# Another order of the same calls in the step functions of VectorE, ScalarE and GpSimd

## The chip, the cores and the metric

One Trainium2 chip, one core. The metric is the device time of one execution in microseconds.

## The reference

Tokens are 8 sequences of 2048 rows with 512 channels, float32. First an attention-like recurrence with a residual and a layer norm, then a gated feed-forward with token shift, a residual and a second layer norm:

```
rkv = x @ W_rkv + b_rkv;  r, k, v = split(rkv)
k = exp(k);  kv = k * v
y = associative_scan(y[t] = lam * y[t-1] + [kv, k][t]);  u1, u2 = split(y)
a = (u1 + gamma * kv) / (u2 + gamma * k + 1e-6) * sigmoid(r)
x = layernorm(x + a @ W_o + b_o)
x_prev = x shifted by one token, zero at the start of a sequence
xr = mu_r * x + (1 - mu_r) * x_prev;  xk = mu_k * x + (1 - mu_k) * x_prev
o = sigmoid(xr @ W_r.T) * (square(relu(xk @ W_k.T)) @ W_v.T)
out = layernorm(x + o)
```

## The kernel before

The 16384 tokens are worked in 32 blocks of 512. A block's attention part is computed with channels on the partitions, in four chunks of 128 channels (`c` = 0 to 3), and its feed-forward part in two halves of 256 tokens (`half` 0 and 1), tiles of 128 tokens with tokens on the partitions. Every operand of a product is held as a high part (`_hi`, rounded by ScalarE) and a low part (`_lo`, the difference, by VectorE or GpSimd), and each product is three matmuls: high by high, high by low, low by high. A projection is 12 matmuls (L787 to L789) into one of four banks `bankA`; the output, receptance and value products (L804 to L806), the transposes (L830) and the key products (L852 to L854) go into four banks `bankB`, taken in a fixed rotation (`SLOTS`): each product waits until the engine that reads the one four slots before it is done.

The work is pipelined by hand: a step `s` holds the attention part of block `s`, the output product and most of the feed-forward part of block `s - 1` (`s1`), and the value product of half 1 with the last norm of block `s - 2` (`s2`). Each of the five engines has its own `step` function that says in which order it calls the pieces; they synchronise by semaphores alone. Steps 0 to 2 are straight code, then a hardware loop runs over batches 1 to 7 with four steps in its body, then step 31, `last_block` and `last_half`. An engine takes its instructions in the order written; one that waits holds up all behind it.

TensorE's step is: projections of chunk 0; value product of half 1 of `s2`; output products of `s1` (four tiles); first projection of chunk 1; two transposes of half 0; the rest of chunks 1 and 2; two transposes of half 1; receptance and key products of half 0; projections of chunk 3; value, receptance and key products of half 0, 1 and 1.

The pieces that the change moves, and what they wait for:

- ScalarE: `exp_key` (L434) and `exp_gate` (L440, L443) read a projection; `att_high` (L447) waits for GpSimd's `att`; `copy_zT` (L455) empties two transposes' banks; `previous_scaled` (L463) makes eight chunks from `zT`; `mixed_high` (L483) waits for VectorE's `mix`; `normalise` (L470) waits for GpSimd's `inverse_std` (`shift`, L334); `tanh` (L495) empties a receptance bank; `key_square` (L505 to L509) empties a key bank and makes `ka_f`, `ka_hi`; `x_high` (L415) waits for the load of the next block's `xT`.
- VectorE: `denominator` (L633 to L651), `numerator` (L659 to L664), `attention_rows` (L685), `statistics` (L671, L677), `mix` (L694), `key_low` (L702), `gated_values` (L710), `x_low` (L607).
- GpSimd: `att` (L316), `att_low` (L320), `inverse_std` (L325 to L334), `mixed_low` (L341), `residual` (L347), `bias_rows` (L353), and in step 0 `weight_low` (L311).
- SyncE's queue issues the loads and stores in a fixed order: store of half 1 of `s2` (after its `normalise`), row loads of half 1, `xT` of block `s + 1` (after the last projection), row loads of half 0, store of half 0 of `s1`.

Of the kernel before, what the change touches and what calls it, by code (L numbers as in the profile page):

```python
# [86 lines left out]
def program(nc, xT, x, w_rkv, w_o, w_r, w_k, w_v, b_rkv, b_o, nu_log, gamma_log, mu_r, mu_k, out, seq):  # L87
# [9 lines left out]
    with ExitStack() as ctx:  # L97
# [199 lines left out]
        def _(pool):  # L297
# [57 lines left out]
            def step(s):  # L355
                s1, s2 = s.back(1), s.back(2)
                first = s.batch is None and s.s == 0
                if s2.exists():
                    residual(s2, 1)
                if s1.exists():  # L360
                    inverse_std(s1, 0, 0)
                if s2.exists():
                    inverse_std(s2, 1, 1)
# [8 lines left out]
                att(s, 1)  # L372
                att_low(s, 1)
                if first:
                    weight_low(W_R)
                att(s, 2)
                att_low(s, 2)
                if first:
                    weight_low(W_K)
                if s1.exists():  # L380
                    mixed_low(s1, 1, s)
                    residual(s1, 0)
                att(s, 3)
# [3 lines left out]
                if s1.exists():  # L387
                    inverse_std(s1, 1, 0)
                bias_rows(s)

            def last_block(s):
                s1, s2 = s.back(1), s.back(2)
# [16 lines left out]
        def _(act):  # L409
# [116 lines left out]
            def step(s):  # L526
                s1 = s.back(1)
# [8 lines left out]
                if s.back(2).exists():  # L536
                    normalise(s.back(2), 1, 1, result_rows(s.back(2)), out_made)
                if s1.exists():
                    copy_zT(s1, 0)
                    normalise(s1, 0, 1, z_rows(s1), z_made)  # L540
                    previous_scaled(s1, 0, s)
                att_high(s, 0)
                exp_gate(s, 1)
                if first:
                    weight_high(W_R)
                if s1.exists():
                    mixed_high(s1, 0, s)
                exp_key(s, 2)
# [12 lines left out]
                exp_key(s, 3)  # L561
# [5 lines left out]
                if s.back(-1).exists() and not first:  # L567
                    x_high(s.back(-1))
                att_high(s, 3)
                if s1.exists():  # L570
                    normalise(s1, 1, 0, result_rows(s1), out_made)
                    tanh(s1, 1)
                    key_square(s1, 1)

            def last_block(s):
                s1, s2 = s.back(1), s.back(2)
# [379 lines left out]
```

## Time and profile before

| | |
|---|---|
| median of 3 runs | 2697.14 us (2694.0 to 2699.29) |
| profiled execution, its own time | 2699.09 us |
| its span | 2697.3 us |
| mean granted TensorE clock | 0.987 |
| instructions | 36409 |

The profile is one execution. Its page gives each engine's busy time; the waits say who waited for whom and how long; the timeline lists instructions in order of time, those that follow each other at the same line in one row; the windows give busy time and the granted clock in a stretch. Idle time of an engine that doesn't bound the kernel costs nothing by itself.

### The profile page before, as it was taken

How to read it: one execution, taken by the hardware profiler on the slowest of the kernel's cores; microseconds unless marked ns; L12 is line 12 of the kernel's file. 1: busy time of each engine (PE TensorE's matmuls, PEld its weight loads, DVE VectorE, ACT ScalarE, POOL GpSimd, SP SyncE). 2: the span in 40 equal slices, each digit the busy share in tenths (PEclk: the TensorE clock that was granted, in tenths of full speed). 3: DMA queues.
4: the chain of work that ended last, by engine and by line, in shares of the span. 5: the costliest groups of instructions: out<-in, count | busy, mean ns of one | idle time of the engine just before them, and what ended most of it. 6: DMA issues, size and time to landing. Idle time of an engine off the chain costs nothing.

```text
span 2697.3 us, 36409 instructions
## 1 busy us (share of the span) xinstructions
PE 2560.1 (95%) x12800; PEld 2166.3 (80%) x12800; DVE 2045.1 (76%) x2826; ACT 1287.5 (48%) x2255; POOL 1293.9 (48%) x1166
## 2 busy tenths in 40 slices
PE   7899999999999999999999999999999999999997
PEld 5788888878888888888888888888888888888886
DVE  8877778777778777877777777777877777777773
ACT  4445454544454444545454544445454444545454
POOL 3545454454554454454544544545445454454453
PEclk8999999999999999999999999999999999999998
DMA  4001111011010011110111100111101111101010
GB/s 168 16 32 48 32 48 40 24 48 48 32 48 32 33 47 36 44 40 27 46 48 32 48 32 32 47 32 48 40 24 47 48 33 40 39 32 47 32 32 24
DMA packets 57800, 110.89 MB, mean 41 GB/s; under 512 B 7040, under 2 KB 7040, under 8 KB 57088
## 3 DMA queue, kind: packets, MB, share of 16 engines
q1 hardware_dynamic: 57600, 108.31, 12.1%
q8 instruction: 115, 1.88, 0.3%
q14 instruction: 85, 0.70, 0.1%
HBM read 74.73 MB, written 33.55 MB: 40 GB/s over the span
## 4 chain that ended last, share of the span: by engine, by line
PE 47%; DVE 20%; ACT 13%; issue 12%; POOL 7%; DMA 1%; SPq 0%; DVEq 0%; ACTq 0%; POOLq 0%
PE bankB L804 8%; PE bankB L806 7%; PE bankB L805 7%; PE bankA L787 5%; PE bankA L789 5%; PE bankA L788 5%; DVE gate L648 4%; DVE x_lo L607 4%; POOL att_f L316 4%; PE bankB L852 3%; PE bankB L853 3%; PE bankB L854 3%; DVE att_f L659 3%; ACT t L470 2%; ACT xr_f L463 2%
## 5 line engine op out<-in xcount | busy, mean ns | idle before, releaser
L787 PE MATMUL bankA<-x_hi,wrkv_hi 128*128 128x512 f32 x1536 | 606.7, 395 | 26.2 <-DVE x_lo L607 11.4
L788 PE MATMUL bankA<-x_lo,wrkv_hi 128*128 128x512 f32 x1536 | 602.5, 392 | 0.0
L789 PE MATMUL bankA<-x_hi,wrkv_lo 128*128 128x512 f32 x1536 | 601.9, 392 | 0.0
L651 DVE RECIPROCAL gate<-gate 128x512 f32<-128x512 f32 x128 | 429.2, 3353 | 4.4
L316 POOL TENSOR_TENSOR att_f<-att_f,gate 128x512 f32<-128x512 f32 x128 | 205.2, 1603 | 381.5 <-DVE att_f L664 380.7
L320 POOL TENSOR_TENSOR att_lo<-att_f,att_hi 128x512 fp32r<-128x512 f32 x128 | 205.8, 1608 | 358.2 <-ACT att_hi L447 358.2
L787 PEld LDWEIGHTS bankA<-x_hi,wrkv_hi 128*128 128x128 f32 x1536 | 291.1, 190 | 87.8 <-issue 23.1
L852 PE MATMUL bankB<-xk_hi,wk_hi 128*128 128x256 f32 x1024 | 297.4, 290 | 64.7 <-ACT zT L455 58.9
L702 DVE TENSOR_TENSOR ka_lo<-ka_f,ka_hi 128x512 fp32r<-128x512 f32 x128 | 104.6, 817 | 334.4 <-ACT ka_f L509 334.4
L789 PEld LDWEIGHTS bankA<-x_hi,wrkv_lo 128*128 128x128 f32 x1536 | 290.8, 189 | 61.6
L347 POOL TENSOR_TENSOR t<-t,y 128x512 f32<-128x512 f32 x128 | 191.2, 1514 | 304.3 <-DVE t L710 304.3
L788 PEld LDWEIGHTS bankA<-x_lo,wrkv_hi 128*128 128x128 f32 x1536 | 291.1, 190 | 57.1
L447 ACT ACTIVATE att_hi<-att_f 128x512 fp32r<-128x512 f32 x128 | 80.1, 626 | 474.3 <-POOL att_f L316 474.3
L470 ACT ACTIVATE y<-y,shift,rstd 128x512 f32<-128x512 f32 x128 | 97.2, 810 | 436.8 <-POOL shift L334 436.7
L853 PE MATMUL bankB<-xk_lo,wk_hi 128*128 128x256 f32 x1024 | 294.0, 287 | 0.0
L854 PE MATMUL bankB<-xk_hi,wk_lo 128*128 128x256 f32 x1024 | 293.7, 287 | 0.0
L852 PEld LDWEIGHTS bankB<-xk_hi,wk_hi 128*128 128x128 f32 x1024 | 200.4, 196 | 79.8 <-ACT zT L455 76.3
L804 PE MATMUL bankB<-wv_hi,ka_hi 128*128 128x512 f32 x512 | 201.4, 393 | 19.3 <-DVE ka_lo L702 18.5
L341 POOL TENSOR_TENSOR xr_lo<-xr_f,xr_hi 128x1024 fp32r<-128x1024 f32 x64 | 166.6, 2603 | 110.3 <-ACT xr_hi L483 110.0
L804 PE MATMUL bankB<-wo_hi,att_hi 128*128 128x512 f32 x512 | 201.1, 393 | 11.9 <-POOL att_lo L320 9.9
L804 PE MATMUL bankB<-wr_hi,xr_hi 128*128 128x512 f32 x512 | 202.0, 395 | 0.0
L853 PEld LDWEIGHTS bankB<-xk_lo,wk_hi 128*128 128x128 f32 x1024 | 200.9, 196 | 1.2
(88 smaller groups left out, 5720.3 us busy)
## 6 DMA issues: line engine op xcount, KB each, us to landing
x_f<-in_xT SPq DMA_DIRECT2D x128, 256.0 KB, 4.0
y<-in_x SPq DMA_DIRECT2D x128, 256.0 KB, 2.7
out<-t SPq DMA_DIRECT2D x128, 256.0 KB, 2.0
wrkv_f<-in_w_rkv SPq DMA_DIRECT2D x3, 768.0 KB, 6.3
wo_f<-in_w_o SPq DMA_DIRECT2D x1, 1024.0 KB, 9.7
wr_f<-in_w_r SPq DMA_DIRECT2D x1, 1024.0 KB, 11.6
wk_f<-in_w_k SPq DMA_DIRECT2D x1, 1024.0 KB, 13.6
wv_f<-in_w_v SPq DMA_DIRECT2D x1, 1024.0 KB, 15.6
```

Of the source, the lines that this page charges most:

```text
L316: pool.tensor_tensor(att_f[:, c], att_f[:, c], gate[:, c % 2], ALU.mult).then_inc(att_made, 1)
L320: pool.tensor_tensor(att_lo[:, c], att_f[:, c], att_hi[:, c], ALU.subtract).then_inc(att_lo_made, 1)
L347: pool.tensor_tensor(t[:, tile], t[:, tile], y[:, y_slot(s, tile)], ALU.add).then_inc(y2_made, 1)
L651: dve.reciprocal(gate[:, c % 2], gate[:, c % 2]).then_inc(rec_made, 1)
L787: pe.matmul(bank[:], w_hi, x_hi[:, h], start=(h == 0), stop=False)
L788: pe.matmul(bank[:], w_hi, x_lo[:, h], start=False, stop=False)
L789: last = pe.matmul(bank[:], w_lo, x_hi[:, h], start=False, stop=(h == NC - 1))
L804: pe.matmul(bank[:], hi, w_hi[:, c], start=(c == 0), stop=False)
L805: pe.matmul(bank[:], hi, w_lo[:, c], start=False, stop=False)
L852: pe.matmul(dst, wk_hi[:, c, cols], xk_hi[:, c], start=(c == 0), stop=False)
L853: pe.matmul(dst, wk_hi[:, c, cols], xk_lo[:, c], start=False, stop=False)
L854: last = pe.matmul(dst, wk_lo[:, c, cols], xk_hi[:, c], start=False, stop=(c == NC - 1))
```

## The change

The `step` and `last_block` functions of VectorE, ScalarE and GpSimd call the same pieces with the same arguments in another order. SyncE's functions are untouched. TensorE's `step` has its loops over `which` written out as three calls each, in the same order. No instruction is added or removed. The tuple's parentheses and `(not first)` in the diff change nothing and are left out below, as is the text of TensorE's.

```diff
 GpSimd
             def step(s):
+                if s1.exists():
+                    inverse_std(s1, 0, 0)
                 if s2.exists():
                     residual(s2, 1)
-                if s1.exists():
-                    inverse_std(s1, 0, 0)
-                if s2.exists():
-                    inverse_std(s2, 1, 1)
                 if s1.exists():
                     inverse_std(s1, 0, 1)
                 att(s, 0)
...
                 att(s, 1)
+                if s2.exists():
+                    inverse_std(s2, 1, 1)
                 att_low(s, 1)
                 if first:
                     weight_low(W_R)
                 att(s, 2)
+                if s1.exists():
+                    mixed_low(s1, 1, s)
+                    residual(s1, 0)
                 att_low(s, 2)
                 if first:
                     weight_low(W_K)
-                if s1.exists():
-                    mixed_low(s1, 1, s)
-                    residual(s1, 0)
                 att(s, 3)
+                if s1.exists():
+                    inverse_std(s1, 1, 0)
                 att_low(s, 3)
                 if first:
                     weight_low(W_V)
-                if s1.exists():
-                    inverse_std(s1, 1, 0)
                 bias_rows(s)
             def last_block(s):
                 inverse_std(s1, 0, 0)
                 residual(s2, 1)
+                inverse_std(s2, 1, 1)
                 inverse_std(s1, 0, 1)
-                inverse_std(s2, 1, 1)
 ScalarE
             def step(s):
...
                     normalise(s1, 0, 0, z_rows(s1), z_made)
                 exp_key(s, 1)
-                if s.back(2).exists():
-                    normalise(s.back(2), 1, 1, result_rows(s.back(2)), out_made)
                 if s1.exists():
                     copy_zT(s1, 0)
-                    normalise(s1, 0, 1, z_rows(s1), z_made)
                     previous_scaled(s1, 0, s)
-                att_high(s, 0)
+                    mixed_high(s1, 0, s)
                 exp_gate(s, 1)
                 if first:
                     weight_high(W_R)
-                if s1.exists():
-                    mixed_high(s1, 0, s)
+                att_high(s, 0)
                 exp_key(s, 2)
+                if s1.exists():
+                    normalise(s1, 0, 1, z_rows(s1), z_made)
                 exp_gate(s, 2)
+                if s1.exists():
+                    copy_zT(s1, 1)
                 att_high(s, 1)
                 if first:
                     weight_high(W_K)
                 if s1.exists():
-                    copy_zT(s1, 1)
+                    key_square(s1, 0)
+                if s.back(2).exists():
+                    normalise(s.back(2), 1, 1, result_rows(s.back(2)), out_made)
+                if s1.exists():
+                    previous_scaled(s1, 1, s)
+                exp_key(s, 3)
+                if s1.exists():
                     tanh(s1, 0)
-                    key_square(s1, 0)
-                    previous_scaled(s1, 1, s)
-                if first:
-                    x_high(s.back(-1))
-                att_high(s, 2)
-                exp_key(s, 3)
                 exp_gate(s, 3)
                 if first:
                     weight_high(W_V)
                 if s1.exists():
                     mixed_high(s1, 1, s)
-                if s.back(-1).exists() and not first:
+                att_high(s, 2)
+                if first:
+                    x_high(s.back(-1))
+                if s.back(-1).exists() and (not first):
                     x_high(s.back(-1))
                 att_high(s, 3)
                 if s1.exists():
-                    normalise(s1, 1, 0, result_rows(s1), out_made)
                     tanh(s1, 1)
                     key_square(s1, 1)
+                    normalise(s1, 1, 0, result_rows(s1), out_made)
             def last_block(s):
                 normalise(s1, 0, 0, z_rows(s1), z_made)
                 copy_zT(s1, 0)
                 previous_scaled(s1, 0, s)
+                mixed_high(s1, 0, s)
+                normalise(s2, 1, 1, result_rows(s2), out_made)
                 normalise(s1, 0, 1, z_rows(s1), z_made)
-                normalise(s2, 1, 1, result_rows(s2), out_made)
-                mixed_high(s1, 0, s)
                 copy_zT(s1, 1)
                 key_square(s1, 0)
+                previous_scaled(s1, 1, s)
                 tanh(s1, 0)
-                previous_scaled(s1, 1, s)
                 mixed_high(s1, 1, s)
+                normalise(s1, 1, 0, result_rows(s1), out_made)
                 key_square(s1, 1)
                 tanh(s1, 1)
-                normalise(s1, 1, 0, result_rows(s1), out_made)
 VectorE
             def step(s):
...
                     attention_rows(s1, 0)
-                if s2.exists():
-                    statistics(s2, 1, 1, result_rows(s2), y2_made)
-                if s1.exists():
                     attention_rows(s1, 1)
                 numerator(s, 0)
                 if s1.exists():
                     mix(s1, 0, s)
                 denominator(s, 1)
+                if s2.exists():
+                    statistics(s2, 1, 1, result_rows(s2), y2_made)
                 numerator(s, 1)
...
-                if first:
-                    x_low(s.back(-1))
                 denominator(s, 3)
                 if s1.exists():
                     gated_values(s1, 0)
+                if first:
+                    x_low(s.back(-1))
...
             def last_block(s):
                 attention_rows(s1, 0)
                 gated_values(s2, 1)
-                attention_rows(s1, 1)
                 statistics(s2, 1, 1, result_rows(s2), y2_made)
                 mix(s1, 0, s)
+                attention_rows(s1, 1)
```

Where the instructions stand, at three places. First ScalarE in step 3, from the end of `exp_gate(s, 2)` to `exp_key(s, 3)`, before:

```order
L443 ACTIVATE gate<-gate 128x512
L447 ACTIVATE att_hi<-att_f 128x512
L455 ACTIVATE zT<-bankB 128x2x256 x2
L495 ACTIVATE t<-bankB 128x512 x2
L505 ACTIVATE ka_f<-bankB 128x512
...
L463 ACTIVATE xr_f<-zT,om_mu 128x256 x4
L463 ACTIVATE xk_f<-zT,om_mu 128x256 x4
L447 ACTIVATE att_hi<-att_f 128x512
L434 ACTIVATE key<-bankA,b_sb 128x512
```

and of the change:

```order
L443 ACTIVATE gate<-gate 128x512
L455 ACTIVATE zT<-bankB 128x2x256 x2
L447 ACTIVATE att_hi<-att_f 128x512
L505 ACTIVATE ka_f<-bankB 128x512
...
L470 ACTIVATE t<-t,shift,rstd 128x512 x2
L463 ACTIVATE xr_f<-zT,om_mu 128x256 x4
L463 ACTIVATE xk_f<-zT,om_mu 128x256 x4
L434 ACTIVATE key<-bankA,b_sb 128x512
L495 ACTIVATE t<-bankB 128x512 x2
```

The copy of the transposed rows (`zT`) moved ahead of `att_hi`; tanh (`t` from `bankB`) moved from behind the copy to behind `key`; the scaling of two result tiles (L470) came in ahead of the eight chunks.

Second, ScalarE at the end of the same step, before:

```order
L415 ACTIVATE x_hi<-x_f 128x512 x4
L447 ACTIVATE att_hi<-att_f 128x512
L470 ACTIVATE t<-t,shift,rstd 128x512 x2
L495 ACTIVATE t<-bankB 128x512 x2
L505 ACTIVATE ka_f<-bankB 128x512
```

and of the change:

```order
L415 ACTIVATE x_hi<-x_f 128x512 x4
L447 ACTIVATE att_hi<-att_f 128x512
L495 ACTIVATE t<-bankB 128x512 x2
L505 ACTIVATE ka_f<-bankB 128x512
...
L470 ACTIVATE t<-t,shift,rstd 128x512 x2
```

The scaling of the half's two result tiles went from ahead of tanh and the squares to the end of the step.

Third, VectorE in step 0, from the end of `numerator(s, 2)` to the end of `denominator(s, 3)`, before:

```order
L664 SCALAR_TENSOR_TENSOR att_f<-kv,gamma,att_f 128x512
L607 TENSOR_TENSOR x_lo<-x_f,x_hi 128x512 x4
L633 SCALAR_TENSOR_TENSOR u<-lam,key 128x512
L638 SCALAR_TENSOR_TENSOR kv<-bankA,b_sb,key 128x512
...
L651 RECIPROCAL gate<-gate 128x512
```

and of the change:

```order
L664 SCALAR_TENSOR_TENSOR att_f<-kv,gamma,att_f 128x512
L633 SCALAR_TENSOR_TENSOR u<-lam,key 128x512
L638 SCALAR_TENSOR_TENSOR kv<-bankA,b_sb,key 128x512
...
L651 RECIPROCAL gate<-gate 128x512
L607 TENSOR_TENSOR x_lo<-x_f,x_hi 128x512 x4
```

The low parts of the next block's `xT` went from ahead of the last denominator to behind it.

## Rows read from the trace of the kernel before

**Rows 1.** The page, part 1: busy time, share of the span, instructions of each engine.

```profile
PE 2560.1 (95%) x12800; PEld 2166.3 (80%) x12800; DVE 2045.1 (76%) x2826; ACT 1287.5 (48%) x2255; POOL 1293.9 (48%) x1166
```

**Rows 2.** TensorE's waits: engine, line, who ended them; us, times, longest.

```profile
PE bankB L852 <- ACT zT L455: 58.9, 31, 2.1
PE bankB L804 <- DVE ka_lo L702: 18.5, 23, 0.8
```

**Rows 3.** Timeline of TensorE: start, duration (us), line, operation, [idle before it].

```profile
1377.61 0.40 PE L787 MATMUL bankA<-x_hi,wrkv_hi 128*128 128x512 f32 x1
...
1386.73 0.47 PE L804 MATMUL bankB<-wv_hi,ka_hi 128*128 128x512 f32 x1 [0.77 <-DVE ka_lo L702]
...
1426.48 0.39 PE L806 MATMUL bankB<-wr_hi,xr_lo 128*128 128x512 f32 x1
1428.83 0.38 PE L852 MATMUL bankB<-xk_hi,wk_hi 128*128 128x256 f32 x1 [1.96 <-ACT zT L455]
...
1434.67 0.40 PE L787 MATMUL bankA<-x_hi,wrkv_hi 128*128 128x512 f32 x1
...
1442.86 0.39 PE L804 MATMUL bankB<-wv_hi,ka_hi 128*128 128x512 f32 x1
...
1453.74 0.28 PE L852 MATMUL bankB<-xk_hi,wk_hi 128*128 128x256 f32 x1
...
1459.49 0.40 PE L787 MATMUL bankA<-x_hi,wrkv_hi 128*128 128x512 f32 x1
```

**Rows 4.** Timeline of ScalarE and GpSimd, same step, around the key products.

```profile
1419.30 2.85 POOL L341 TENSOR_TENSOR xk_lo<-xk_f,xk_hi 128x1024 fp32r<-128x1024 f32 x1
...
1427.66 0.63 ACT L447 ACTIVATE att_hi<-att_f 128x512 fp32r<-128x512 f32 x1 [5.73 <-POOL att_f L316]
1428.19 1.07 ACT L455 ACTIVATE zT<-bankB 128x512 f32<-128x512 f32 x2
...
1436.71 1.70 ACT L463 ACTIVATE xr_f<-zT,om_mu 128x256 f32<-128x256 f32 x4
...
1439.91 0.62 ACT L447 ACTIVATE att_hi<-att_f 128x512 fp32r<-128x512 f32 x1
```

**Rows 5.** Timeline of ScalarE and VectorE before the value product of half 1.

```profile
1379.74 1.52 ACT L470 ACTIVATE t<-t,shift,rstd 128x512 f32<-128x512 f32 x2 [2.71 <-POOL shift L334]
1381.16 1.06 ACT L495 ACTIVATE t<-bankB 128x512 f32<-128x512 f32 x2
...
1385.89 0.69 DVE L702 TENSOR_TENSOR ka_lo<-ka_f,ka_hi 128x512 fp32r<-128x512 f32 x1 [0.64 <-ACT ka_f L509]
```

**Rows 6.** Windows over key products: busy PE, PEld, DVE, ACT, POOL; PEclk; DMA.

```profile
1263.00:1271.00 8.00, 7.39 (x49) 7.40 (x50) 6.82 (x6) 3.88 (x8) 2.98 (x2) 0.79 0.00 0
...
1346.00:1353.00 7.00, 6.07 (x49) 6.05 (x50) 6.86 (x7) 4.21 (x9) 2.16 (x2) 1.00 0.01 2
```

**Rows 7.** Timeline of VectorE in step 0, TensorE's output product in step 1.

```profile
31.80 5.15 DVE L648 SCALAR_TENSOR_TENSOR gate<-key,gate 128x512 f32<-128x512 f32 x1 [1.46 <-ACT gate L443]
...
57.91 0.69 DVE L607 TENSOR_TENSOR x_lo<-x_f,x_hi 128x512 fp32r<-128x512 f32 x1 [1.36 <-ACT x_hi L415]
59.01 1.82 DVE L633 TENSOR_TENSOR_SCAN u<-lam,key 128x512 f32<-128x512 f32 x1 [0.41 <-ACT key L434]
...
75.38 0.79 PE L804 MATMUL bankB<-wo_hi,att_hi 128*128 128x512 f32 x1 [9.88 <-POOL att_lo L320]
```

**Rows 8.** Timeline of TensorE at the begin of the last block.

```profile
2619.39 0.64 PE L804 MATMUL bankB<-wo_hi,att_hi 128*128 128x512 f32 x1 [2.06 <-ACT ka_f L505]
```

**Rows 9.** Timeline of VectorE: the low parts of the next block's input.

```profile
1449.66 5.12 DVE L607 TENSOR_TENSOR x_lo<-x_f,x_hi 128x512 fp32r<-128x512 f32 x4
```

**Rows 10.** Timeline of GpSimd and VectorE at the same time.

```profile
1416.52 2.82 POOL L341 TENSOR_TENSOR xr_lo<-xr_f,xr_hi 128x1024 fp32r<-128x1024 f32 x1
...
1417.12 2.77 DVE L648 SCALAR_TENSOR_TENSOR gate<-key,gate 128x512 f32<-128x512 f32 x1
```

**Rows 11.** Timeline of GpSimd: the product of chunk 1.

```profile
1425.43 2.19 POOL L316 TENSOR_TENSOR att_f<-att_f,gate 128x512 f32<-128x512 f32 x1 [3.29 <-DVE att_f L664]
```

More of the change, by code:

```diff
@@ L355, in step @@
             def step(s):
-                s1, s2 = s.back(1), s.back(2)
+                s1, s2 = (s.back(1), s.back(2))
                 first = s.batch is None and s.s == 0
-                if s2.exists():
-                    residual(s2, 1)
                 if s1.exists():
@@ L362, in step @@
                 if s2.exists():
-                    inverse_std(s2, 1, 1)
+                    residual(s2, 1)
                 if s1.exists():
@@ L379, in step @@
                     weight_low(W_K)
+                att(s, 3)
                 if s1.exists():
-                    mixed_low(s1, 1, s)
-                    residual(s1, 0)
-                att(s, 3)
+                    inverse_std(s1, 1, 0)
                 att_low(s, 3)
@@ L386, in step @@
                     weight_low(W_V)
-                if s1.exists():
-                    inverse_std(s1, 1, 0)
                 bias_rows(s)
             def last_block(s):
-                s1, s2 = s.back(1), s.back(2)
+                s1, s2 = (s.back(1), s.back(2))
                 inverse_std(s1, 0, 0)
                 residual(s2, 1)
+                inverse_std(s2, 1, 1)
                 inverse_std(s1, 0, 1)
-                inverse_std(s2, 1, 1)
                 mixed_low(s1, 0, s)
@@ L545, in step @@
                     weight_high(W_R)
+                att_high(s, 0)
+                exp_key(s, 2)
                 if s1.exists():
-                    mixed_high(s1, 0, s)
-                exp_key(s, 2)
+                    normalise(s1, 0, 1, z_rows(s1), z_made)
                 exp_gate(s, 2)
+                if s1.exists():
+                    copy_zT(s1, 1)
                 att_high(s, 1)
@@ L570, in step @@
                 if s1.exists():
-                    normalise(s1, 1, 0, result_rows(s1), out_made)
                     tanh(s1, 1)
                     key_square(s1, 1)
+                    normalise(s1, 1, 0, result_rows(s1), out_made)
             def last_block(s):
-                s1, s2 = s.back(1), s.back(2)
+                s1, s2 = (s.back(1), s.back(2))
                 normalise(s1, 0, 0, z_rows(s1), z_made)
@@ L716, in step @@
             def step(s):
-                s1, s2 = s.back(1), s.back(2)
+                s1, s2 = (s.back(1), s.back(2))
                 first = s.batch is None and s.s == 0
@@ L742, in step @@
                     gated_values(s1, 0)
-                if s.back(-1).exists() and not first:
+                if first:
+                    x_low(s.back(-1))
+                if s.back(-1).exists() and (not first):
                     x_low(s.back(-1))
@@ L750, in last_block @@
             def last_block(s):
-                s1, s2 = s.back(1), s.back(2)
+                s1, s2 = (s.back(1), s.back(2))
                 attention_rows(s1, 0)
                 gated_values(s2, 1)
-                attention_rows(s1, 1)
                 statistics(s2, 1, 1, result_rows(s2), y2_made)
                 mix(s1, 0, s)
+                attention_rows(s1, 1)
                 key_low(s1, 0)
@@ L865, in step @@
             def step(s):
-                s1, s2 = s.back(1), s.back(2)
-                for which in range(3):
-                    project(s, 0, which)
+                s1, s2 = (s.back(1), s.back(2))
+                project(s, 0, 0)
+                project(s, 0, 1)
+                project(s, 0, 2)
                 if s2.exists():
@@ L878, in step @@
                 project(s, 1, 2)
-                for which in range(3):
-                    project(s, 2, which)
+                project(s, 2, 0)
+                project(s, 2, 1)
+                project(s, 2, 2)
                 if s1.exists():
@@ L884, in step @@
                     keys(s1, 0, s)
-                for which in range(3):
-                    project(s, 3, which)
+                project(s, 3, 0)
+                project(s, 3, 1)
+                project(s, 3, 2)
                 if s1.exists():
@@ L892, in last_block @@
             def last_block(s):
-                s1, s2 = s.back(1), s.back(2)
+                s1, s2 = (s.back(1), s.back(2))
                 attention_out(s1, 0, s)
```

## The prediction

> **What bounds the kernel now.** I read the page first: TensorE is busy 95% of the span, VectorE 76%, ScalarE and GpSimd 48% each [rows 1]. A new order on the three others can win only what TensorE stands idle, 137 us, plus what its stalls cost around them. So the next view is who ends TensorE's waits. Two groups recur in every step: 58.9 us in 31 waits before the first key product, put down to ScalarE's copy of transposed rows (L455), and 18.5 us in 23 waits before a value product, put down to VectorE's `ka_lo` (L702) [rows 2]. Third, one ordinary step in TensorE's timeline [rows 3]: it lasts 1459.49 - 1377.61 = 81.88 us and holds exactly these two stalls, 0.77 and 1.96 us. I found no other idle time in it.
>
> A stall costs more than its idle time. The key product starts 2.35 us after the last receptance matmul (1426.48 to 1428.83), where the 48 matmuls from 1442.86 to 1453.74 start 0.23 us apart: 2.12 us lost for 1.96 idle. Its group then takes 5.84 us (to 1434.67), where the unstalled one takes 5.75 (1453.74 to 1459.49). I take 0.25 us on top of every idle stretch.
>
> **The change, part by part.** It adds and removes no instruction, and TensorE's order is the same. So the sum is stalls that go, less stalls that come.
>
> 1. *Key product, half 0.* It needs the bank of the third transpose, so `copy_zT(s1, 1)`. Before, that copy stands on ScalarE behind `att_high(s, 1)`, which sat idle 5.73 us for GpSimd's `att_f` and ran at 1427.66; the copy follows at 1428.19, the product at 1428.83 [rows 3, 4]. The transposes lie one receptance group ahead of the product, 24 matmuls or 5.4 us. Now the copy stands ahead of `att_high(s, 1)`, right behind `exp_gate(s, 2)`, and can end 3 to 4 us before the product wants it. What is late next is `xk_lo`, on GpSimd at 1419.30 for 2.85 us, 4.5 us before the product's natural start at 1426.7. So this wait goes: 58.9 + 31 x 0.25 = **66.7 us**.
>
> 2. *Value product, half 1.* Before, ScalarE sat idle 2.71 us behind `att_high(s, 3)` for GpSimd's shift, scaled two result tiles (1.42 us to the next start), and only then tanh and the squares that `ka_lo` needs; `ka_lo` began at 1385.89 and the product at 1386.73 [rows 3, 5]. With the scaling behind the squares, these start 2.71 + 1.42 = 4.1 us earlier, against a product that wants them 0.8 us earlier and, by item 1, follows the previous key product at the same distance. 3 us are left. 18.5 + 23 x 0.25 = **24.3 us**.
>
> 3. *Clock.* In four of the seven steps that begin a batch, the window over the stalled key product shows a granted clock of 0.79 against 1.00 in an ordinary step, that is a part at 1.2 GHz and the rest at 2.4, and the same 49 matmuls are busy 7.39 us, not 6.07 [rows 6]. TensorE had just stood idle for 2 us. With the stall gone I expect no fall: 4 x 1.3 = **5.3 us**.
>
> 4. *First step.* It is bound by VectorE's chain, not by TensorE: the output product waits 9.88 us for the last `att_lo`, at 75.38 [rows 7]. Two things shorten that chain. `exp_gate(s, 1)` no longer stands behind `att_high(s, 0)`, so VectorE's gate multiplication (1.46 us idle, then 5.15 us beside GpSimd's `wo_lo`) starts before `wo_lo`; its following scan may still lie beside it, so of 6.6 us some 3.8 are won. And `x_low` for the next block, which ended at 58.60 with 1.36 us idle in it, moves behind `denominator(s, 3)`, whose own start at 59.01 so comes some 5 us earlier. The chain gains about 8 us; the first projections of the next step now start later behind it and take back 1 to 2. I take **6.5 us**, between 0 (another wait takes over) and 10.
>
> 5. *Last blocks.* The output product waited 2.06 us for `ka_f` [rows 8], which item 2 brings forward: 2.3. In the last block `mixed_high(s1, 0)` moves ahead of two scalings that wait for GpSimd, but `tanh(s1, 0)` goes behind `previous_scaled(s1, 1)` and `key_square(s1, 1)` behind a scaling, which costs some of it again: I take **6 us** in all (0 to 9), since the stalled products there also run partly at the lower clock.
>
> *What is made later, and its cover.* `normalise(s2, 1, 1)` now stands between the squares of half 0 and `previous_scaled(s1, 1)`, 1.42 us more in that queue; `exp_key(s, 3)` moves ahead of tanh. The place where it can bite is the value product of half 0, whose bank tanh must free. Counted from the start of chunk 3's projections (1434.67): the second squares end and the next operation starts at +2.04 (1436.71), scaling 1.42, eight chunks 3.20 (1436.71 to 1439.91), `exp_key` at most 0.67, one tanh of the pair's 1.06 some 0.6: +7.9 [rows 3 to 5]. The product's natural start is +8.19 (1442.86). Slack 0.3 us: I cost it at nothing. The DVE side of the same delay ends in `x_lo`, which before was done at 1454.78, 4.7 us ahead of the next projection [rows 9]; it comes about 1 us later relative to TensorE. On SyncE the store of half 1, its row loads and then the load of the next block's `xT` stand in this order; the store now goes out near +3.5, ahead of the +8.2 at which `xT` may go, so it holds nothing up. GpSimd's `residual(s2, 1)` moves behind one small group, `att_low(s, 2)` behind the two mixed differences; both have until the next step.
>
> *Shared time of VectorE and GpSimd.* Gate multiplication took 2.77 us where GpSimd ran `xr_lo` (2.82 us) beside it [rows 10]; an operation of this size takes 0.69 undisturbed, as `ka_lo` [rows 5]. In the new order it starts before GpSimd's operation, so I expect less of this there, and VectorE's 2045.1 / 32 = 63.9 us a step against a period of 78.65 leave room. The Trainium skill, "GPSIMD Engine Reference", section on key points, says that GpSimd shares its SBUF interfaces with VectorE and collides with VectorE instructions that read two SBUF inputs. The row agrees. By that rule every new pairing may cost as much as this one; the sum would be that of the second rival below.
>
> Sum: 66.7 + 24.3 + 5.3 + 6.5 + 6 = 108.8. The profiled execution has a time of 2699.1 (its span is 1.8 shorter): 2590.3, taken as **2590**. The median of the runs shown is 2 us below that execution, which I leave aside. The period should be 81.88 - 2.21 - 1.02 = 78.65 us. Bounds of this case: with nothing from items 4 and 5, 2603; with their best, 2584. Its own range is 2578 to 2608. A measurement of this kernel can tell about 0.2%, some 5 us, from no change.
>
> **The rivals.**
> *Tanh is late (0.15).* The slack of 0.3 us is less than one waiting instruction. If ScalarE's chain is 1 us longer, 31 value products wait: 31 x (0.7 + 0.25) = 29 us, 2619. For it: the chain really is back to back. Against: every piece is measured, and it hangs on the same key product.
>
> *VectorE collides with GpSimd anew (0.13).* If `statistics(s2, 1, 1)` and the mixes fall beside GpSimd's large differences and two of them stretch as the gate did, by 2.1 us each, with the 1 us of above and 1 for the scan, VectorE is 6 us late, `x_lo` 1.3 us too late: 31 x (1.3 + 0.25) = 48 us, 2638.
>
> *Nothing is won (0.03).* The reorder doesn't free the key product: the copy comes early, but `mixed_low(s1, 0)` slips 4.5 + 2 us on GpSimd behind a later `att_high(s, 0)`, and the product waits as long for `xk_lo`. About 2697.
>
> *Slower (0.05).* `normalise(s2, 1, 1)` waits for GpSimd's shift, now queued behind `att(s, 1)`, and everything behind it on ScalarE waits too. Before, that `att` ended at 1427.62 [rows 11]; at most 2.7 us more give the shift, 1430.3, and the scaling's place is 1436.7: 6.4 us of slack. If VectorE's chain (residual, statistics, `numerator(s, 1)`) came 11 us later than this, the value product would wait 31 x (11 - 6.4 - 0.3 + 0.25) = 141 us: 2731. It decides from 10 us, where the whole gain is eaten. Against: that chain has no such length, and the copy and tanh free the same engines earlier.
>
> **How the numbers follow.** Forecast 0.64 at 2590, tanh 0.15, collision 0.13, nothing 0.03, slower 0.05. The range takes the forecast's own and reaches over the tanh case and most of the way to the collision: 2576 to 2632. Faster by over 0.2%: 0.64 + 0.15 + 0.13 = 0.92, and 0.01 of the third case, where less than all is lost, 0.93; within 0.2%: 0.02; slower: 0.05.
>
> **What would show it.** In the waits: no TensorE row for L455 and `ka_lo` beyond a few us, `att_lo` below 8. In TensorE's timeline a period near 78.65 us, and the key product of half 0 with 0.23 us before it. ScalarE: the copy at least 3 us ahead of that product. In the windows: granted clock 1.00 in the key products at batch begins. I'd be wrong on the middle if a row "value product waits for `t`, L495" stands there, on the collision if `x_lo` ends TensorE's waits in every step, and on item 4 if the output product of the second step doesn't start before 70 us.

## The result and the profile after

The changed kernel takes **2582.32 us** (median of 4 runs, 2582.24 to 2583.88), the kernel before, in the same comparison, 2698.22 us (2694.0 to 2701.23). The ratio is 0.9573, 95% interval 0.9556 to 0.9589: 116 us less, where the forecast was 2590 (109 less) in a range of 2576 to 2632. The profiled execution has a time of 2583.88 and a span of 2582.1 us.

TensorE's lines stand two further down now (L789 for L787, L806 for L804, L854 for L852), VectorE's three. The page's first part, against [rows 1]:

```profile
PE 2531.9 (98%) x12800; PEld 2160.3 (84%) x12800; DVE 2044.4 (79%) x2826; ACT 1293.9 (50%) x2255; POOL 1318.1 (51%) x1166
```

TensorE's idle time fell from 2697.3 - 2560.1 = 137.2 to 50.2 us: 87.0. Its busy time fell by 28.2 us for the same 12800 matmuls. Together that is the 115.2 us of the span. A forecast by idle time alone would have missed a quarter.

TensorE's waits, against [rows 2] (engine, line, who ended them: us, times, longest):

```profile
PE bankA L789 <- DVE x_lo L610: 20.1, 2, 13.6
PE bankA L789 <- issue: 9.7, 6, 2.0
PE bankB L832 <- ACT y L470: 5.8, 2, 5.3
PE bankA L789 <- DVE kv L641: 2.8, 1, 2.8
PE bankB L806 <- ACT t L495: 2.3, 1, 2.3
...
PE bankB L806 <- DVE ka_lo L705: 0.2, 1, 0.2
```

The row for L455 and the one with 23 waits for `ka_lo` are gone, and no recurring row took their place. What is left occurs once or twice, but for the six waits on "issue": there are six jumps back in the hardware loop.

An ordinary step in TensorE's timeline, against [rows 3] (start, duration, line, operation, [idle before it]):

```profile
1321.04 0.40 PE L789 MATMUL bankA<-x_hi,wrkv_hi 128*128 128x512 f32 x1
...
1329.23 0.39 PE L806 MATMUL bankB<-wv_hi,ka_hi 128*128 128x512 f32 x1
...
1368.89 0.39 PE L808 MATMUL bankB<-wr_hi,xr_lo 128*128 128x512 f32 x1
1369.12 0.28 PE L854 MATMUL bankB<-xk_hi,wk_hi 128*128 128x256 f32 x1
...
1374.87 0.40 PE L789 MATMUL bankA<-x_hi,wrkv_hi 128*128 128x512 f32 x1
...
1383.06 0.39 PE L806 MATMUL bankB<-wv_hi,ka_hi 128*128 128x512 f32 x1
...
1399.69 0.40 PE L789 MATMUL bankA<-x_hi,wrkv_hi 128*128 128x512 f32 x1
```

The period is 1399.69 - 1321.04 = 78.65 us, as forecast. The key product of half 0 starts 0.23 us after the matmul before it (2.35 before), the value product of half 1 waits for nothing.

ScalarE in the same step, against [rows 4, 5]:

```profile
1320.94 0.63 ACT L447 ACTIVATE att_hi<-att_f 128x512 fp32r<-128x512 f32 x1 [10.06 <-POOL att_f L316]
1321.48 1.07 ACT L495 ACTIVATE t<-bankB 128x512 f32<-128x512 f32 x2
...
1364.25 1.07 ACT L455 ACTIVATE zT<-bankB 128x512 f32<-128x512 f32 x2
1368.12 0.63 ACT L447 ACTIVATE att_hi<-att_f 128x512 fp32r<-128x512 f32 x1 [2.80 <-POOL att_f L316]
...
1382.09 1.06 ACT L495 ACTIVATE t<-bankB 128x512 f32<-128x512 f32 x2
```

The copy ends at 1365.3, 3.8 us ahead of the key product. `att_hi` still waits, but nothing that TensorE needs soon stands behind it. At the other end tanh begins with no scaling ahead of it, right behind `att_hi`. The tight place is the last row: the first tanh of the pair ends near 1382.7, the value product of half 0, whose bank it empties, begins at 1383.06.

VectorE and GpSimd, against [rows 9, 10] (one timeline each):

```profile
1326.22 0.97 DVE L705 TENSOR_TENSOR ka_lo<-ka_f,ka_hi 128x512 fp32r<-128x512 f32 x1 [0.74 <-ACT ka_f L509]
...
1357.19 0.69 DVE L651 SCALAR_TENSOR_TENSOR gate<-key,gate 128x512 f32<-128x512 f32 x1
...
1362.61 2.22 DVE L662 TENSOR_TENSOR_SCAN att_f<-lam,carry,kv 128x512 f32<-128x512 f32 x1
...
1390.11 5.97 DVE L610 TENSOR_TENSOR x_lo<-x_f,x_hi 128x512 fp32r<-128x512 f32 x4
```

```profile
1358.99 2.40 POOL L341 TENSOR_TENSOR xr_lo<-xr_f,xr_hi 128x1024 fp32r<-128x1024 f32 x1
1361.36 2.38 POOL L341 TENSOR_TENSOR xk_lo<-xk_f,xk_hi 128x1024 fp32r<-128x1024 f32 x1
```

The gate multiplication now ends ahead of `xr_lo` and takes 0.69 us (2.77 in [rows 10]). A collision remains further on: the scan beside `xk_lo` takes 2.22 us, where one with nothing beside it takes 1.2. `ka_lo` ends 2.0 us ahead of its product (1327.19 to 1329.23), `x_lo` 3.6 us ahead of the next projection (1396.08 to 1399.69).

Two windows of TensorE's clock, against [rows 6] (busy PE, PEld, DVE, ACT, POOL; PEclk; DMA):

```profile
1211.00:1219.00 8.00, 8.00 (x60) 7.59 (x59) 7.01 (x7) 3.50 (x6) 4.44 (x6) 1.00 0.00 0
1797.00:1805.00 8.00, 8.00 (x29) 6.39 (x29) 3.91 (x5) 4.77 (x8) 6.12 (x5) 0.79 0.21 74
```

The first is a key product at a batch begin: granted clock 1.00, where it was 0.79 before. The second lies right behind a loop jump whose pause was 1.99 us: there the clock still falls. Of the six jumps in this trace two do this (pauses of 1.97 and 1.99 us) and the four with 1.34 to 1.63 us idle don't; the last section has jumps of other runs that don't fit this split. Counted between key products of half 0, the six periods with a jump take 80.3 to 80.5 us where it doesn't fall and 82.5 where it does, all others 78.64 to 78.67.

The head, against [rows 7], and the last block (TensorE):

```profile
60.08 0.76 PE L789 MATMUL bankA<-x_hi,wrkv_hi 128*128 128x512 f32 x1 [13.59 <-DVE x_lo L610]
...
70.22 0.39 PE L806 MATMUL bankB<-wo_hi,att_hi 128*128 128x512 f32 x1
...
2550.60 0.50 PE L806 MATMUL bankB<-wv_hi,ka_hi 128*128 128x512 f32 x1 [2.27 <-ACT t L495]
```

The output product of the second step starts at 70.22 instead of 75.38 and waits for nothing: the whole wait is at `x_lo` now. In the last block the value product waits 2.27 us for `tanh(s1, 0)`, which now stands behind the eight chunks of `previous_scaled(s1, 1)`.

### The profile page after: what moved, and what is told of

Read it like the earlier page. It is cut to its first block, busy times and chain, and to the rows that moved or that the text cites. A ratio compares the mean times of both kernels' runs of the same rounds, so it can differ in the third digit from the quotient of the medians.

```text
span 2582.1 us, 36409 instructions
## 1 busy us (share of the span) xinstructions
PE 2531.9 (98%) x12800; PEld 2160.3 (84%) x12800; DVE 2044.4 (79%) x2826; ACT 1293.9 (50%) x2255; POOL 1318.1 (51%) x1166
## 3 DMA queue, kind: packets, MB, share of 16 engines
q1 hardware_dynamic: 57600, 108.31, 12.5%
## 4 chain that ended last, share of the span: by engine, by line
PE 96%; DVE 1%; issue 1%; POOL 1%; ACT 0%; DMA 0%; SPq 0%; ACTq 0%; POOLq 0%
PE bankB L806 13%; PE bankB L808 13%; PE bankB L807 13%; PE bankA L789 13%; PE bankA L790 13%; PE bankA L791 13%; PE bankB L854 5%; PE bankB L856 5%; PE bankB L855 5%; PE bankB L832 2%; DMA wrkv_f<-in_w_rkv 0%; DVE att_f L662 0%; DVE gate L654 0%; POOL t L347 0%; DVE st L674 0%
## 5 line engine op out<-in xcount | busy, mean ns | idle before, releaser
L789 PE MATMUL bankA<-x_hi,wrkv_hi 128*128 128x512 f32 x1536 | 606.6, 395 | 32.7 <-DVE x_lo L610 20.1
L789 PEld LDWEIGHTS bankA<-x_hi,wrkv_hi 128*128 128x128 f32 x1536 | 291.0, 189 | 93.1 <-issue 31.7
L470 ACT ACTIVATE y<-y,shift,rstd 128x512 f32<-128x512 f32 x128 | 97.0, 806 | 413.2 <-POOL shift L334 413.2
L341 POOL TENSOR_TENSOR xr_lo<-xr_f,xr_hi 128x1024 fp32r<-128x1024 f32 x64 | 153.9, 2405 | 282.0 <-ACT xr_hi L483 282.0
L325 POOL TENSOR_TENSOR ve<-mv,eps_ln 128x2 f32<-128x2 f32 x128 | 65.5, 511 | 448.1 <-DVE mv L680 448.1
L854 PE MATMUL bankB<-xk_hi,wk_hi 128*128 128x256 f32 x1024 | 290.8, 284 | 0.0
L320 POOL TENSOR_TENSOR att_lo<-att_f,att_hi 128x512 fp32r<-128x512 f32 x128 | 185.8, 1452 | 192.3 <-ACT att_hi L447 192.3
L705 DVE TENSOR_TENSOR ka_lo<-ka_f,ka_hi 128x512 fp32r<-128x512 f32 x128 | 109.9, 859 | 199.4 <-ACT ka_f L509 199.3
L688 DVE TENSOR_TENSOR y<-bankB,y 128x512 f32<-128x512 f32 x128 | 88.2, 691 | 177.4 <-PE bankB L808 177.0
L353 POOL TENSOR_TENSOR y<-y,bo 128x512 f32<-128x512 f32 x128 | 212.5, 1692 | 0.0
L806 PE MATMUL bankB<-wr_hi,xr_hi 128*128 128x512 f32 x512 | 202.3, 395 | 0.0
L806 PE MATMUL bankB<-wv_hi,ka_hi 128*128 128x512 f32 x512 | 199.6, 390 | 2.5 <-ACT t L495 2.3
L808 PE MATMUL bankB<-wr_hi,xr_lo 128*128 128x512 f32 x512 | 199.7, 390 | 0.0
```

Of the source, the lines that this page charges most:

```text
L353: pool.tensor_tensor(rows, rows, bo[:], ALU.add).then_inc(y_biased, 1)
L789: pe.matmul(bank[:], w_hi, x_hi[:, h], start=(h == 0), stop=False)
L806: pe.matmul(bank[:], hi, w_hi[:, c], start=(c == 0), stop=False)
L808: last = pe.matmul(bank[:], lo, w_hi[:, c], start=False, stop=(c == NC - 1))
L854: pe.matmul(dst, wk_hi[:, c, cols], xk_hi[:, c], start=(c == 0), stop=False)
```

## The experiments

**Is each of the two stalls worth its price alone?** The sum added a price for the key product's stall and one for the value product's. Three kernels, each the kernel before with one call moved, or both.

```diff
 e1_copy_first (before, ScalarE's step)
                 exp_gate(s, 2)
+                if s1.exists():
+                    copy_zT(s1, 1)
                 att_high(s, 1)
...
                 if s1.exists():
-                    copy_zT(s1, 1)
                     tanh(s1, 0)
```

> The kernel before, with one pair exchanged on ScalarE: copy_zT(s1, 1) stands ahead of att_high(s, 1), all else as before. Theory of the queue place (the key product waits because the copy stands behind a waiting instruction): its 58.9 us of waits go, with 31 x 0.25 us around them and the lower clock of four batch begins (5.3): 72 us less, near 2626, and the wait of the value product for ka_lo (18.5 us) stays. Rival (another producer, xk_lo, ends that wait next): less than 20 us gained.

Measured: 2736.9 us (2731.9 to 2738.7), ratio 1.0129 (1.0106 to 1.0152): 1.3% **slower** than before, where 2626 was expected, though the stall it aimed at is gone. The page's first part:

```profile
PE 2591.3 (95%) x12800; PEld 2193.5 (80%) x12800; DVE 2127.5 (78%) x2826; ACT 1287.8 (47%) x2255; POOL 1305.6 (48%) x1166
```

TensorE's first wait:

```profile
PE bankB L805 <- DVE ka_lo L703: 83.9, 29, 3.5
```

One step's value product, and the spacing of its matmuls:

```profile
656.26 0.76 PE L805 MATMUL bankB<-wv_hi,ka_hi 128*128 128x512 f32 x1 [3.43 <-DVE ka_lo L703]
656.82 0.63 PE L806 MATMUL bankB<-wv_lo,ka_hi 128*128 128x512 f32 x1
```

The wait for `ka_lo` grew from 0.77 to 3.43 us. From the value product of half 0 to the end of the last `ka_lo` it was 25.6 us before (1360.98 to 1386.58) and is 28.3 (627.85 to 656.11). First the kernel before (TensorE, VectorE; the last `ka_lo` is in [rows 5]):

```profile
1360.98 0.39 PE L804 MATMUL bankB<-wv_hi,ka_hi 128*128 128x512 f32 x1
1362.64 0.69 DVE L648 SCALAR_TENSOR_TENSOR gate<-key,gate 128x512 f32<-128x512 f32 x1
```

and e1 (TensorE, VectorE and GpSimd):

```profile
627.85 0.39 PE L805 MATMUL bankB<-wv_hi,ka_hi 128*128 128x512 f32 x1
630.43 2.64 POOL L341 TENSOR_TENSOR xr_lo<-xr_f,xr_hi 128x1024 fp32r<-128x1024 f32 x1 [3.32 <-ACT xr_hi L483]
630.84 2.77 DVE L649 SCALAR_TENSOR_TENSOR gate<-key,gate 128x512 f32<-128x512 f32 x1
...
655.42 0.69 DVE L703 TENSOR_TENSOR ka_lo<-ka_f,ka_hi 128x512 fp32r<-128x512 f32 x1 [0.65 <-ACT ka_f L509]
```

The 2.7 us have two parts of about the same size. TensorE came earlier and VectorE's chain did not: VectorE reaches the gate multiplication 3.0 us behind the start of the value product, where it was 1.7. And the multiplication now falls beside a difference of GpSimd and takes 2.77 us, not 0.69; the four `x_lo` behind it take 0.8 less (5.10 before, 4.32 now). So one half of the growth is the time that TensorE gained, and the other a collision that this order brings with it. No run separates the two.

Behind the stall the matmuls start 0.43 us apart instead of 0.23, and the window 656 to 664 us has a granted clock of 0.62. Against the kernel before the span grew by 39.6 us, of which idle time is only 145.6 - 137.2 = 8.4; 31.2 us are the same matmuls, slower. So the stall moved one product on and grew, and the lower clock made most of the loss.

```diff
 e2_norm_last (before, ScalarE's step)
                 att_high(s, 3)
                 if s1.exists():
-                    normalise(s1, 1, 0, result_rows(s1), out_made)
                     tanh(s1, 1)
                     key_square(s1, 1)
+                    normalise(s1, 1, 0, result_rows(s1), out_made)
```

> The kernel before, with normalise(s1, 1, 0) on ScalarE moved behind tanh and key_square of half 1 at the end of the step. Theory: the value product no longer waits for ka_lo: 24 us less, near 2674, and the key product waits as before (about 59 us). The granted clock in the key products of batch begins stays near 0.8 if it is that stall that lowers it. Rival (that stall is covered by another one, so nothing moves): 2697.

Measured: 2696.3 us (2687.3 to 2698.9, 10 runs), ratio 0.9978 (0.9966 to 0.9991). TensorE's first wait:

```profile
PE bankB L852 <- ACT zT L455: 58.9, 31, 2.0
```

A window over a key product in an ordinary step:

```profile
686.00:694.00 8.00, 7.25 (x48) 7.26 (x49) 6.76 (x7) 4.01 (x8) 2.97 (x2) 0.79 0.01 2
```

No wait for `ka_lo` is left, and idle time fell by 20.1 us (2685.5 - 2568.4 = 117.1). But busy time rose by 8.3 in this execution, the fastest of the ten: the key product, still stalled for 2 us, now runs partly at the lower clock in 18 of 31 steps (0.79 in the window), ordinary ones among them, and then takes 7.34 us (686.75 to 694.09), not 5.84. Before it did so in 4 of 31, all in steps that follow a jump. The expected 24 us came out as 4 in the medians.

**e3_both** makes both moves.

> Both exchanges of the two runs beside it, in the kernel before. Theory: they are independent and add up: 72 + 24 = 96 us less, near 2602, with the steps at 78.65 us; what is then left to the changed kernel's 2582 is its first step and its last blocks (about 17 us). Rival (the rest of the new order in the steps is needed too): steps longer than 79 us and a time above 2615.

Measured: 2602.7 us (2602.4 to 2603.5), ratio 0.9639 (0.9619 to 0.9659). As expected, neither stall is left; the ordinary periods are 78.65 to 79.0 us. Alone +36 and -4 us on the same kernel before (2700.6 in this comparison), together -98: the two prices are right as a pair and wrong one by one. These two calls carry most of the change. Its other moves are worth 18.5 us more (profiled spans 2600.6 and 2582.1). By the traces 7.7 of them lie ahead of the first key product (113.14 and 105.46), 7.1 behind the one of half 0 at 2490.97 (2479.58 in the changed kernel), and 3.7 in the steps between.

**Which of the change's moves frees the key product?**

```diff
 e4_undo_copy (changed kernel, ScalarE's step)
                 exp_gate(s, 2)
-                if s1.exists():
-                    copy_zT(s1, 1)
                 att_high(s, 1)
...
                 if s1.exists():
+                    copy_zT(s1, 1)
                     key_square(s1, 0)
```

> The changed kernel with copy_zT(s1, 1) put back behind att_high(s, 1). Theory of the queue place alone: the whole stall returns, 31 x 2.2 us and some lower clock, near 2650. Rival (the chain that att_high waits for comes earlier in the new order too, so that the stall has two remedies): att_high(s, 1) ends at 1368.75 in the trace of the changed kernel, the copy would end about 0.55 later, at 1369.3, and the product's natural start is 1369.1: 0.2 to 0.4 us a step, near 2597.

Measured: 2588.6 us (2588.1 to 2589.9), ratio 0.9587 (0.9567 to 0.9607). ScalarE and TensorE around the key product:

```profile
1371.88 0.63 ACT L447 ACTIVATE att_hi<-att_f 128x512 fp32r<-128x512 f32 x1 [3.79 <-POOL att_f L316]
1372.41 1.07 ACT L455 ACTIVATE zT<-bankB 128x512 f32<-128x512 f32 x2
```

```profile
1372.65 0.39 PE L807 MATMUL bankB<-wr_hi,xr_lo 128*128 128x512 f32 x1
1373.05 0.39 PE L853 MATMUL bankB<-xk_hi,wk_hi 128*128 128x256 f32 x1
```

The copy is back behind `att_high(s, 1)`, yet the product starts only 0.40 us after the matmul before it instead of 0.23 (0.22 to 0.42 over the steps), and its group takes 5.85 us, not 5.75. In the new order GpSimd's `att` itself is ready earlier: `att_hi` starts 1.0 us ahead of the product's natural start (1368.12 against 1369.12 in the changed kernel), where before it started 1.0 us behind it (1427.66 against 1426.7). The copy's place is worth 6 us there, not 67. The key product's stall has two remedies: the copy's place removes it alone (e1), the earlier `att` nearly does. Which of the moved calls makes `att` earlier was not tested.

**How thin is tanh's slack?**

```diff
 e5_tanh_behind_gate (changed kernel, ScalarE's step)
                 exp_key(s, 3)
+                exp_gate(s, 3)
                 if s1.exists():
                     tanh(s1, 0)
-                exp_gate(s, 3)
```

> The changed kernel with tanh(s1, 0) moved behind exp_gate(s, 3) on ScalarE. In the trace of the changed kernel the value product of half 0 begins at 1383.06 and tanh at 1382.09; behind exp_gate (1383.26 to 1384.6) the first tanh would end near 1385.1, 2.0 us after the product's natural start. Theory of the prediction (slack 0.3 to 0.4 us, then every us costs a us and 0.25 around it): 31 x 2.25 = 70 us more, near 2652, and up to 30 x 1.5 us more where the granted clock falls behind the stall. Rival (the place isn't tight, another wait covers it): below 2590.

Measured: 2679.7 us (2673.6 to 2692.3, 8 runs), ratio 0.9937 (0.992 to 0.9955). TensorE's first wait:

```profile
PE bankB L806 <- ACT t L495: 61.9, 32, 2.3
```

In the changed kernel this row has 2.3, so 59.6 us are new. The span is 89.7 us longer, idle time 59.2 of it, busy time 30.5. Between the key products of half 0 the granted clock falls in 12 of 30 periods. One call one place later costs 97 of the 116 us gained (expected were 70 and up to 45 more by the clock).

**e10_norm_back** undoes the other of the two moves, `normalise(s1, 1, 0)`, in the changed kernel: the diff of e2 the other way round.

> The changed kernel with normalise(s1, 1, 0) put back ahead of tanh and key_square of half 1. In the trace of the changed kernel ka_lo ends at 1327.2, the value product's natural start is 1329.2; the scaling would wait for the shift until 1322.4 and move tanh from 1321.5 to 1323.9: ka_lo 2.4 us later, 0.4 us too late. Theory (slacks add up along ScalarE's queue): 31 x (0.4 + 0.25) = 20 us more, near 2602. Rival (as in the kernel before with the copy alone moved, the stall grows to 3 us): above 2640. Second rival (covered): 2582.

Measured: 2602.1 us (2599.4 to 2604.2), ratio 0.965 (0.9631 to 0.9668).

```profile
PE bankB L806 <- DVE ka_lo L705: 11.6, 24, 0.5
```

As expected, two us of slack less the delay of the scaling leave a wait of half a microsecond; ordinary periods are 79.3 to 79.5 us. So a short stall costs its 0.5 and some 0.3 around it, and no fall of the clock stands behind it (0.994 over the whole execution).

**Head and tail by themselves.** e6_old_first_step gives step 0 its old order and leaves the others alone, e7_old_last_block does that for `last_block` on all three engines.

```diff
 e6_old_first_step (changed kernel: ScalarE, VectorE; x_high and att_high(s, 2) likewise, ahead of exp_key(s, 3))
+                if first:
+                    att_high(s, 0)
                 exp_gate(s, 1)
                 if first:
                     weight_high(W_R)
-                att_high(s, 0)
+                if not first:
+                    att_high(s, 0)
...
+                if first:
+                    x_low(s.back(-1))
                 denominator(s, 3)
                 if s1.exists():
                     gated_values(s1, 0)
-                if first:
-                    x_low(s.back(-1))
```

> The changed kernel with the old order in step 0 alone (att_high(s, 0) ahead of exp_gate(s, 1), x_high and att_high(s, 2) ahead of exp_key(s, 3), x_low ahead of denominator(s, 3)). Theory: the first step's part of the gain is undone and nothing else: 8 us more, near 2590, and step 2 begins near 144 us, not 136. Rival (the steps behind it take up the difference): 2582.

Measured: 2590.3 us (2589.2 to 2590.5), ratio 0.9603 (0.9586 to 0.962): 8.0 us more than the changed kernel. The old wait for `att_lo` is back, 9.7 us, step 2 begins at 143.12 us instead of 136.03, and the ordinary periods stay as they are.

```diff
 e7_old_last_block (changed kernel; ScalarE's part)
                 previous_scaled(s1, 0, s)
-                mixed_high(s1, 0, s)
-                normalise(s2, 1, 1, result_rows(s2), out_made)
                 normalise(s1, 0, 1, z_rows(s1), z_made)
+                normalise(s2, 1, 1, result_rows(s2), out_made)
+                mixed_high(s1, 0, s)
...
-                previous_scaled(s1, 1, s)
                 tanh(s1, 0)
+                previous_scaled(s1, 1, s)
                 mixed_high(s1, 1, s)
-                normalise(s1, 1, 0, result_rows(s1), out_made)
                 key_square(s1, 1)
                 tanh(s1, 1)
+                normalise(s1, 1, 0, result_rows(s1), out_made)
```

> The changed kernel with the old last_block on all three engines. From the last key product of step 31 on, the changed kernel is 8.2 us shorter than the kernel before. Theory: about 4 of them are the stall for ka_f and the lower clock behind it, which end with the order in the step and stay; the other 4 are last_block's, so 2586. Rival (the late tanh in the new last_block, a 2.3 us stall, eats what mixed_high's place wins): within 1 us of 2582.

Measured: 2587.4 us (2585.7 to 2588.2), ratio 0.9594 (0.9576 to 0.9611): 5.1 us more. In the traces the part from the last ordinary key product of half 0 to the end takes 107.2 us (from 2477.64) instead of 102.5 (from 2479.58), 4.6 more; about 4 were expected. The wait for `xk_lo` of 5.8 us is back, that for `t` gone.

**Can the jumps go?** What recurs in the changed kernel is the loop. e8_straight writes all 32 steps out.

```diff
 e8_straight (changed kernel)
-            for s in range(per_batch - 1):
+            for s in range(blocks):
                 step(Step(per_batch, s=s, blocks=blocks))
-            with eng.Fori(1, batches) as batch:
-                for j in range(-1, per_batch - 1):
-                    step(Step(per_batch, batch=batch, j=j, blocks=blocks))
-            step(Step(per_batch, s=blocks - 1, blocks=blocks))
```

> The changed kernel with its loop over batches written out as straight code (the same steps in the same order, waits on constants). In the trace of the changed kernel the six steps that follow a jump back are 1.9, 1.7, 1.6, 1.6, 3.9 and 3.8 us longer than the others, 14.5 us in all, the last two with a lower granted clock. Theory: the jump is the cause of all of it, so 2568 and every step 78.65 us. Rival (long straight code makes waits of its own for instructions): 2582 or more, with waits put down to issue spread over the steps.

Measured: **2569.8 us** (2569.4 to 2570.9), ratio 0.9528 (0.951 to 0.9546), the fastest of all, 12.5 us under the changed kernel.

```profile
PE 2526.3 (98%) x12800; PEld 2156.5 (84%) x12800; DVE 2044.8 (80%) x2826; ACT 1287.8 (50%) x2255; POOL 1326.7 (52%) x1166
```

Every period is 78.63 to 78.67 us. The jumps' extra over their neighbours was 1.9 + 1.7 + 1.6 + 1.6 + 3.9 + 3.8 = 14.5 us, so nearly all of it came back: idle time is 8.8 us less than in the changed kernel, busy time 5.6. No new wait shows in the program written out.

e9_straight_tail is e8 with `tanh(s1, 0)` ahead of `previous_scaled(s1, 1, s)` in `last_block`, against the 2.3 us wait for `t`.

> The same with tanh(s1, 0) put back ahead of previous_scaled(s1, 1) in last_block on ScalarE. The changed kernel's value product there waits 2.27 us for that tanh. Theory: 2.5 us less than the run beside it at the value product, some given back where the eight chunks come later for the next key product: 1 to 2.5 us less, near 2566. Rival: no difference, since the key product then waits for xk_lo as it did in the kernel before (1.93 us).

Measured: 2570.0 us (2569.2 to 2571.9), ratio 0.9529 (0.951 to 0.9547): no difference, where 1 to 2.5 us less were expected.

```profile
PE bankB L850 <- POOL xk_lo L337: 1.9, 1, 1.9
```

This row stands in the place of the wait for `t`: the chunks feed `xk_lo`, which is late instead.

## Why the prediction was right, step by step

**The sum.** 108.8 us were forecast; the medians differ by 115.9, the profiled spans by 115.2. By place: until the second step's successor begins (first projection of step 2 at 145.04 before, 136.03 after) 9.0 us; from there to the last ordinary key product (2611.43 before, 2504.40 after) 107.03 - 9.01 = 98.0; the rest, 8.2, behind it. The forecast had 6.5, 96.3 (items 1 to 3) and 6: all three came out somewhat higher, none covers up an error of another. One thing was luck: the change makes both moves at once. By the same prices e1 was expected at 2626 and came out at 2736.9, e2 at 2674 and came out at 2696.3.

**Items 1 and 2, the stalls.** 66.7 + 24.3 was right as a pair: the period fell from 81.9 to 78.65, the copy ended 3.8 us ahead ("3 to 4"), `ka_lo` 2.0 us ahead of its product, where "3 us are left" was forecast. The reasoning under it was wrong in two points. The sum treated the prices as independent, and "follows the previous key product at the same distance" overlooked that this gain goes to TensorE alone: e1 shows that VectorE's chain does not come earlier with it and even gets longer by a collision, so item 1 without item 2 moves the stall and lengthens it. And item 1's cause was given as the copy's place alone; e4 shows the earlier `att` to be a second, nearly sufficient cause.

**Item 3, the clock.** The key products at batch begins have 1.00, as forecast. Before, four of them took 7.33 to 7.35 us instead of 5.85: 6.0 us in all, where 5.3 were taken, and they are gone. Two other falls the forecast did not see: the kernel before has them behind two of its jumps (pauses of 1.79 and 1.85 us, windows of 0.79), and so has the changed one. Its periods with such a fall are 2 us longer than those with another jump, some 0.5 of it the longer pause itself. Nor was it said why item 2 counts 23 waits and not 31: in the six steps with a jump the pause had hidden the wait for `ka_lo`, and two more, at the start and at the end, stand in other rows. So the six periods with a jump and their successors had 13.9 us over the others before, and have 14.5 after. What the lower clock costs was mainly underrated elsewhere: with one stall of some 2 us or more left it falls in ordinary steps too (e1, e2, e5).

**Item 4, the first step.** 6.5 us taken; 9.0 by place, 8.0 by e6. The mechanism is the one described: the gate multiplication at 30.69 us takes 0.69 instead of 5.15, the scan beside `wo_lo` 3.50. The prediction's own sign, wrong if the output product "doesn't start before 70 us", spoke against this item by 0.22 us (70.22), although its gain had come: the sign was set too tight. The ones to read were that the wait for `att_lo` vanished and that the one for `x_lo` grew to 13.59.

**Item 5, the last blocks.** 6 us taken, 8.2 measured; 5 of them are `last_block`'s own order (e7). The cost of tanh's later place was real, 2.27 us, but e9 shows that moving it back buys nothing.

**Slack.** "0.3 us: I cost it at nothing" was the boldest step. Measured are 0.39 us, in each of the 30 steps from the second on. e5 shows that the tanh rival has the right place: with two operations of 0.69 and 0.63 us and the wait for their projection ahead of tanh, the product waits 1.9 us (31 x 1.9 = 59). With the lower clock each of these waits cost (89.7 - 59.6) / 31 = 1.0 us on top, not 0.25. For a wait as short as the rival's 0.7 us its 0.25 may have been right: the waits of 0.5 us in e10 cost 0.3 on top. No run has one of 0.7 at this place.

**The other rivals.** VectorE's collision with GpSimd did not make TensorE wait in this order: `x_lo` ends 1.1 us nearer to the next projection than before, as forecast, and keeps 3.6. In e1 it did. The Trainium skill, "GPSIMD Engine Reference", section on key points, names VectorE instructions with two SBUF inputs among those that contend with GpSimd. The rows here agree: the gate multiplication reads two and takes 2.77 us beside `xr_lo`, the reciprocal reads one and takes 3.35 us beside `xr_lo` and without it. So it matters what such an operation falls beside: total time in the gate multiplication fell from 158.5 to 90.2 us over its 128 (in e1 it rose to 221.6). `normalise(s2, 1, 1)` does not wait for the shift (it runs at 1376.91, right behind the squares); nor did the case come that nothing is won.

## What to carry to other kernels

Price the stalls of one pipeline together: here a stall that was removed alone handed its time to the next product that hangs on another engine's chain (e1), so ask for each stall how much slack the next one has once this one is gone. Two moves that change the time by -98 us together changed it by +36 and -4 alone, and a trial of one at a time would have thrown out both. When the recurring waits are gone, look at what recurs by the loop itself: writing the steps out gave 12.5 us more.

## What was unexpected of the hardware

- A kernel with a stall of 2.1 us taken out of every step became 1.3% slower, 31 of its 39.6 us by the same matmuls taking longer: behind stalls of 3.1 to 3.4 us the granted clock of 8 us windows was 0.62 to 0.81, and matmuls started 0.43 us apart instead of 0.23. All 23 stalls of 3.1 us or more in the steps of e1 had such a fall behind them, its six of 1.1 to 1.6 us none.
- Stalls of 2 us ran with 1.00 behind them in some steps and 0.79 in others: a fall at 4 of 31 stalled key products before, at 18 of 31 in e2. The length of a pause alone does not decide it. At the loop's jumps, e4 has two pauses of 1.87 us with 1.00 behind them, e6 two of 1.79 and 1.83 with 0.79, and e3 has two of 1.94, one with 0.79 and one with 1.00. What decides it stays open; stalls of 0.5 us (e10) had no fall behind them.
- The loop's jumps cost TensorE 1.34 to 1.99 us of idle time each in the changed kernel; 32 steps of straight code showed no such wait and no other in its place.
